# Row-max pass of an attention stage: next batches' work in half pieces, turns one batch further ahead, one score product issued twice

## What is computed

```python
def _attention(x, qkv_w, qkv_b, proj_w, proj_b):
    B, N, C = x.shape
    hd = C // HEADS                       # 12 heads of 16
    qkv = (x @ qkv_w + qkv_b).reshape(B, N, 3, HEADS, hd).transpose(2, 0, 3, 1, 4)
    q, k, v = (qkv[0], qkv[1], qkv[2])
    attn = jax.nn.softmax(jnp.einsum('bhnd,bhmd->bhnm', q, k) * hd ** (-0.5), axis=-1)
    o = jnp.einsum('bhnm,bhmd->bhnd', attn, v).transpose(0, 2, 1, 3).reshape(B, N, C)
    return o @ proj_w + proj_b
x = x + _attention(_layer_norm(x, ln1_g, ln1_b), qkv_w, qkv_b, proj_w, proj_b)
```

## Time and profile before

| | us |
|---|---|
| Median of 3 runs | 2577.85 (2576.46 to 2578.14) |
| Profiled execution, its own time | 2583.43 |
| Its span in the trace | 2581.4 |
| TensorE busy (matmuls) | 1948.3 (75%) |
| VectorE busy | 1506.0 (58%) |
| ScalarE busy | 1060.0 (41%) |
| Mean granted TensorE clock | 0.803 |

### The profile page before, as it was taken

The page is one execution under the profiler, slowest core; times in us unless marked ns, Lnnn a source line. Parts: engine busy times, 40 slices in busy tenths (PEclk is TensorE's granted clock), DMA queues, the critical chain, the costliest instruction groups (busy, mean ns, idle before and its releaser), DMA issues. The chain is left out here.

```text
span 2581.4 us, 31194 instructions
## 1 busy us (share of the span) xinstructions
PE 1948.3 (75%) x9560; PEld 1011.4 (39%) x9560; DVE 1506.0 (58%) x2508; ACT 1060.0 (41%) x1847; POOL 405.8 (16%) x592
## 2 busy tenths in 40 slices
PE   5687888868876351777568865788899994899994
PEld 4555645444334120000111123333123332788883
DVE  6376378843003665999757774788968886111113
ACT  2001122222111356999878863222167762222221
POOL 5000000000111000111100002522103335122221
PEclk9899989966886565555589986777589997899997
DMA  3011100051992003433000102977767742566664
GB/s 79 18 31 38 46 23 16 11 222 58 392 411 108 12 0 96 145 118 118 25 18 25 36 0 53 126 110 104 94 79 92 97 61 71 176 204 203 204 204 182
DMA packets 147741, 265.16 MB, mean 103 GB/s; under 512 B 28618, under 2 KB 115883, under 8 KB 142636
## 3 DMA queue, kind: packets, MB, share of 16 engines
q1 hardware_dynamic: 135996, 242.54, 36.3%
q0 software_dynamic: 10480, 18.04, 2.1%
q10 hardware_dynamic: 1152, 3.15, 0.3%
HBM read 221.85 MB, written 57.71 MB: 108 GB/s over the span
## 5 line engine op out<-in xcount | busy, mean ns | idle before, releaser
L1646 PE MATMUL ps<-arena 128*128 x384 | 195.8, 615 | 122.1 <-DMA arena<-arena 62.2
L1680 ACT ACTIVATE ps<-ps,arena 128x512 f32<-128x512 f32 x384 | 257.0, 1456 | 7.7 <-POOL arena L1666 7.7
L2091 DVE TENSOR_REDUCE arena<-ps 128x1024 f32 x192 | 227.7, 1222 | 50.4 <-PE ps L2241 44.4
L1656 DVE TENSOR_REDUCE arena<-ps 128x1024 f32 x192 | 234.7, 1226 | 38.1 <-PE ps L1646 22.1
L1680 ACT ACTIVATION_READ_ACCUMULATOR ps<-ps,arena 128x1 f32 x384 | 239.8, 1002 | 0.0
L2443 ACT ACTIVATE arena<-ps 128x1024 f32<-128x1024 f32 x192 | 185.2, 1022 | 95.7 <-PE ps L2325 94.6
L1830 ACT ACTIVATE arena<-ps 128x1024 f32<-128x1024 f32 x192 | 187.5, 1024 | 33.6 <-DVE arena L1852 29.4
L2773 DVE TENSOR_TENSOR arena<-ps,arena 128x384 f32<-128x384 f32 x39 | 21.8, 558 | 286.8 <-PE ps L2729 286.8
L2241 PE MATMUL ps<-arena 96*128 96x512 bf16 x384 | 159.6, 509 | 37.7 <-DVE arena L2091 25.6
L2753 ACT ACTIVATE arena<-ps,arena 128x256 f32<-128x256 f32 x234 | 89.7, 482 | 235.7 <-PE ps L2718 235.7
L528 PE MATMUL ps<-arena 96*128 96x456 f32 (+1 forms) x512 | 177.2, 500 | 9.6 <-DMA arena<-arena 6.1
(11 more groups left out here) (379 smaller groups left out, 3301.4 us busy)
## 6 DMA issues: line engine op xcount, KB each, us to landing
arena<-in_sm_w_dram SPq DMA_DIRECT2D x128, 576.0 KB
arena<-in_re_w_dram SPq DMA_DIRECT2D x39, 1252.0 KB, 5.9
arena<-ra_parts SPq DMA_DIRECT2D x192, 192.0 KB, 9.8
routed_in<-routed_in SPq DMA_DIRECT2D x8, 3332.0 KB, 14.3
ra_parts<-arena SPq DMA_DIRECT2D x48, 192.0 KB, 2.5
arena<-routed_in SPq DMA_DIRECT2D x39, 196.0 KB, 5.3
arena<-la_xt SPq DMA_DIRECT2D x16, 384.0 KB, 3.4
arena<-arena SPq DMA_DIRECT2D x64, 96.0 KB, 2.2
```

The source lines that it names most:

```text
L1646: ins = pe.matmul(ps[:, 2 * (n % 4) + t % 2, :], QM[j][:, h, t * P:(t + 1) * P], KI[:, b, h // HG, :], start=True, stop=True)
L1656: v.tensor_reduce(MXq[:, b, 2 * u:2 * u + 2, at_head(h)], ps[:, 2 * (n % 4):2 * (n % 4) + 2, :], AX.X, ALU.max).then_inc(s_lk, 1)
L1680: ins = act.activation(bank, bank, ACT.Exp, bias=nb[n % 4][:, t % 2:t % 2 + 1], scale=c_reg, accum_out=RS[:, b, t, at_head(h):at_head(h) + 1])
L2091: v.tensor_reduce(MX[:, bass.ds(b, 1), 2 * (n % 2):2 * (n % 2) + 2, n // 2].rearrange("p o t -> p (o t)"), ps[:, 2 * (n % 2):2 * (n % 2) + ...
```

## The change

Seven things are done in the row-max pass; what is computed stays the same.

1. `product` pieces are halved: each covers 256 of the 512 columns, so there are 16 of them. `turn` pieces are halved too (two transposes each).
2. The turns of a batch are made one batch earlier than the rest of its pieces: the pieces that run in batch b are the products and values of b + 2 and the turns of b + 3. The order is 16 half products, two values, four half turns, two values: 24 pieces, one for each unit, from unit 0.
3. The normalisation moves with them: `norm(b + 3)` in round b, with `norm(2)` ahead of the loop. `XT` has two buffers, so a second row is set to one.
4. ScalarE copies the turned rows of b + 1 behind the second part of b, ahead of the values copies of b (`turned`). Its loop is written out.
5. The banks 4 to 7 swap roles from batch to batch (`banks`).
6. In a unit, the first of the two score products is issued twice, into the same bank, but for the units 16, 17, 22 and 23, where the values pieces stand.
7. The first turns stand ahead of the pieces of batches 0 and 1.

```diff
--- before.py
+++ after.py
@@ -1967,7 +1967,7 @@
     Wp, bp = g2(P, [NG, D]), g2(P, [D])
     spare = g2(P, [1])
     mark = g2.at
-    XN, XT = g2(P, [T, D]), g2(DC + 1, [NC, S])
+    XN, XT = g2(P, [T, D]), [g2(DC + 1, [NC, S]) for _ in range(2)]
     QK = [g2(DC, [NC, S]) for _ in range(2)]
     PT = [[g2(DC, [NC, S], BF16) for _ in range(3)] for _ in range(2)]
     W, gb = g2(DC + 1, [NC, 3 * D]), g2(DC, [2, NC])
@@ -2017,7 +2017,8 @@
             l(v.reciprocal(ra, m.wk[2]))
             l(v.tensor_tensor(ra, ra, m.rstd, ALU.mult))
             v.wait_ge(s_w, 16 * (5 + HG))
-            v.memset(XT[DC:DC + 1, 0, :], 1.0)
+            for j in range(2):
+                v.memset(XT[j][DC:DC + 1, 0, :], 1.0)
 
         @block.scalar
         def _(act):
@@ -2036,6 +2037,7 @@
     ld = [sem(f"ra_stacks{j}_loaded") for j in range(2)]
     sl = [sem(f"ra_q_k_shift{j}_loaded") for j in range(2)]
     NLD = 2 * len(PAIRS)
+    banks = lambda b, k: 6 if (b + k) % 2 else 4
     NL2 = NLD + 3
     s_c, s_bt, s_bc = (sem(f"ra_shift_{n}") for n in ("parts", "turned", "copied"))
 
@@ -2094,10 +2096,11 @@
 
             norm(0)
             norm(1)
-            with v.Fori(0, B - 2) as b:
-                norm(b + 2)
+            norm(2)
+            with v.Fori(0, B - 3) as b:
+                norm(b + 3)
                 maxima(b, range(NU))
-            with v.Fori(B - 2, B) as b:
+            with v.Fori(B - 3, B) as b:
                 maxima(b, range(NU))
 
         @block.scalar
@@ -2106,12 +2109,16 @@
                 s.start(act)
             for k in range(2):
                 act.sem_inc(s_wr[k], 1)
-            with act.Fori(0, B) as b:
+
+            def turned(b):
                 xt.wait(act, b, 1)
                 for c in range(NC):
-                    ins = act.activation(XT[0:DC, c, :], ps[0:DC, 4 + c, :], ACT.Identity, bias=gb[:, 1, c:c + 1],
-                                         scale=gb[:, 0, c:c + 1])
+                    ins = act.activation(XT[b % 2][0:DC, c, :], ps[0:DC, banks(b, 0) + c, :], ACT.Identity,
+                                         bias=gb[:, 1, c:c + 1], scale=gb[:, 0, c:c + 1])
                 ins.then_inc(xc.sem, 1)
+
+            turned(0)
+            for b in range(B):
                 for k in range(2):
                     act.wait_ge(s_wr[k], 16 * 3 * b + 1)
                 for s in range(2 * NC):
@@ -2119,17 +2126,19 @@
                     if c == 0:
                         p2.wait(act, b, k - 1)
                     qp.wait(act, b, s + 1)
-                    bank = ps[0:DC, (6, 7, 4, 5)[s], :]
+                    bank = ps[0:DC, banks(b, k) + c, :]
                     act.activation(QK[k][:, c, :], bank, ACT.Copy)
                     act.activation(PT[k][0][:, c, :], bank, ACT.Copy).then_inc(qc.sem, 1)
                 for k in range(2):
                     rest.wait(act, b, k + 1)
                     act.activation(PT[k][1], QK[k], ACT.Copy).then_inc(p1.sem, 1)
+                if b + 1 < B:
+                    turned(b + 1)
                 qp.wait(act, b, 5)
-                Vb = V[:, bass.ds(b, 1), :].rearrange("p o (t h k d) -> p (o t) h k d", t=T, h=NH, k=2)
+                Vb = V[:, b, :].rearrange("p (t h k d) -> p t h k d", t=T, h=NH, k=2)
                 for u in range(2):
-                    ins = act.activation(Vb[:, 2 * u:2 * u + 2, :, 0, :],
-                                         ps[:, 6 + u, 0:2 * D].rearrange("p (t h d) -> p t h d", t=2, h=NH), ACT.Copy)
+                    ins = act.activation(Vb[:, 2 * u:2 * u + 2, :, 0, :], ps[:, banks(b, 0) + u, 0:2 * D].rearrange(
+                        "p (t h d) -> p t h d", t=2, h=NH), ACT.Copy)
                 ins.then_inc(vd.sem, 1)
             for u in range(AHEAD // 2):
                 act.wait_ge(s_bt, u + 1)
@@ -2202,23 +2211,26 @@
                 s.start(pe)
 
 
-            def turn(b, c):
-                if c == 0:
+            def turn(b, c, half):
+                if c == 0 and half == 0:
                     xn.wait(pe, b, 1)
                     qc.wait(pe, b, 0)
-                for t in range(T):
-                    ins = pe.transpose(ps[0:DC, 4 + c, t * P:(t + 1) * P], XN[:, t, c * DC:(c + 1) * DC], m.ident)
-                if c == NC - 1:
+                for t in (2 * half, 2 * half + 1):
+                    ins = pe.transpose(ps[0:DC, banks(b, 0) + c, t * P:(t + 1) * P], XN[:, t, c * DC:(c + 1) * DC],
+                                       m.ident)
+                if c == NC - 1 and half:
                     ins.then_inc(xt.sem, 1)
 
-            def product(b, s, c):
-                if s == 0 and c == 0:
-                    vd.wait(pe, b, 0)
-                    xc.wait(pe, b, 1)
-                rows = DC + 1 - c
-                ins = pe.matmul(ps[0:DC, (6, 7, 4, 5)[s], :], W[0:rows, c, s * DC:(s + 1) * DC], XT[0:rows, c, :],
-                                start=(c == 0), stop=(c == NC - 1))
-                if c == NC - 1:
+            def product(b, s, half, c):
+                if half == 0 and c == 0:
+                    if s == 0:
+                        xc.wait(pe, b, 1)
+                    elif s == NC:
+                        vd.wait(pe, b, 0)
+                rows, part = DC + 1 - c, slice(half * S // 2, (half + 1) * S // 2)
+                ins = pe.matmul(ps[0:DC, banks(b, s // NC) + s % NC, part], W[0:rows, c, s * DC:(s + 1) * DC],
+                                XT[b % 2][0:rows, c, part], start=(c == 0), stop=(c == NC - 1))
+                if half and c == NC - 1:
                     ins.then_inc(qp.sem, 1)
 
             def values(b, t):
@@ -2226,29 +2238,34 @@
                     qc.wait(pe, b, 2)
                 for c in range(NC):
                     rows = DC + 1 - c
-                    ins = pe.matmul(ps[:, 6 + t // 2, t % 2 * D:(t % 2 + 1) * D], XT[0:rows, c, t * P:(t + 1) * P],
-                                    W[0:rows, c, 2 * D:3 * D], start=(c == 0), stop=(c == NC - 1))
+                    ins = pe.matmul(ps[:, banks(b, 0) + t // 2, t % 2 * D:(t % 2 + 1) * D],
+                                    XT[b % 2][0:rows, c, t * P:(t + 1) * P], W[0:rows, c, 2 * D:3 * D],
+                                    start=(c == 0), stop=(c == NC - 1))
                 if t == T - 1:
                     ins.then_inc(qp.sem, 1)
 
-            pieces = [(turn, c) for c in range(NC)] + [(product, s, c) for s in range(2 * NC) for c in range(NC)] + \
-                [(values, t) for t in range(T)]
+            def pieces(b):
+                turns = [(turn, b + 1, c, half) for c in range(NC) for half in range(2)] if b + 1 < B else []
+                return [(product, b, s, half, c) for s in range(2 * NC) for half in range(2) for c in range(NC)] + \
+                    [(values, b, t) for t in range(2)] + turns + [(values, b, t) for t in range(2, T)]
 
             def scores(b, j, n):
                 h = n // 2
                 mx.wait(pe, b, n - 1)
-                for t in (2 * (n % 2), 2 * (n % 2) + 1):
+                first = 2 * (n % 2)
+                for t in (first, first + 1) if n in (16, 17, 22, 23) else (first, first, first + 1):
                     ins = pe.matmul(ps[:, t, :], ST_[j][0][0:KR, h, t * P:(t + 1) * P],
                                     ST_[j][1][0:KR, h, :], start=True, stop=True)
                 ins.then_inc(u1.sem, 1)
 
             def batch(b, ahead):
                 pe.wait_ge(ld[b % 2], 16 * NLD * (b // 2 + 1))
+                work = pieces(b + 2) if ahead else []
                 for n in range(NU):
                     scores(b, b % 2, n)
-                    if ahead and 0 < n <= len(pieces):
-                        piece, *which = pieces[n - 1]
-                        piece(b + 2, *which)
+                    if n < len(work):
+                        piece, *which = work[n]
+                        piece(*which)
                     at = (b - B + 2) * NU + n - 2
                     if 0 <= at < AHEAD * T // 2:
                         if at == 0:
@@ -2260,9 +2277,12 @@
                         if at % T == T - 1:
                             ins.then_inc(s_bt, 1)
 
+            for c in range(NC):
+                for half in range(2):
+                    turn(0, c, half)
             for b in range(2):
-                for piece, *which in pieces:
-                    piece(b, *which)
+                for piece, *which in pieces(b):
+                    piece(*which)
             for b in range(B):
                 batch(b, b + 2 < B)
 
```

## The result

The changed kernel takes 2567.02 us, median of nine runs (2562.74 to 2571.00), against 2578.14, also of nine, for the kernel before: a ratio of 0.9962 (95% interval 0.9951 to 0.9973), some 11 us less. It is faster by more than 0.2%, as forecast, but the gain is under a third of the 37 us expected, and 2567.02 lies outside the range of 2537 to 2556. The profiled execution took 2570.76 us (span 2568.7, mean granted clock 0.817), against 2583.43 (2581.4, 0.803).

What follows compares the result with a forecast made beforehand. The prediction took VectorE to become the bound after the change; its batch terms summed to 226.4 us against 263.4 for the pass, 37.0 us less, so 2577.85 - 37.0 gave 2541 us, range 2537 to 2556.

Steps and rivals of the forecast that it cites:

- its floor: Row-max pass: VectorE's row maximum needs 1.13 us a unit, 27.1 us a batch of 24 units.
- the margin of 0.05 us a unit: All units after the change: room under VectorE's 1.13 us; 0.1 us more per unit would cost 7 us over six batches.
- What was priced at nothing: Row-max pass: extra weight loads, DMA loads and stores, and ScalarE's copies were taken as covered, nothing charged.
- The normalisation, 1.15 us in batches 1 to 4: VectorE's four normalisation instructions, no longer hidden once VectorE is the bound, add 1.15 us to each of batches 1 to 4.
- (batch 0's is before the first score): Batch 0: its normalisation was placed ahead of the first score product, so nothing was charged for it.
- rival 3: Batches 1 to 4: normalisation meets POOL's late subtractions, 3.1 us four times, +12.5 us, 2553.5 us; chance 0.08.
- First batch's low clock, +2.5 us: Batch 0: scores start at clock 0.50, 1.0 us over the floor per unit for 2.5 units, +2.5 us.
- Does the clock hold?: Whole pass: three scores a unit, or two with a piece, were taken to keep TensorE's clock at 1.00.
- Rival 1: Batches 5 to 7: the clock falls and stays low, 1.445 us a unit, +8.5 or +13.5 us; chance 0.22.
- rival 4: Dense part of the batches: the clock stays down and the added columns make it slower, 2612 us; chance 0.03.
- the term of batches 6 and 7 in the sum: Batches 6 and 7: 27.1 and 28.4 us, all units under 1.13 us at 2.4 GHz.
- rival 2: Turn units of every batch: the clock falls there, 2.3 us five times, 12 us, 2553 us; chance 0.07.

Runs made afterwards that it cites:

- E2: Changed kernel with the first score product issued twice in every unit without a values piece, thin units included; ratio to the kernel before 0.9915.
- E1: Changed kernel with VectorE's normalisation moved from the head of the round to behind the twelfth row maximum; ratio to the kernel before 0.9930.
- E10: E5's kernel unchanged, profiled in another execution on the chip of E9; 2561.78 us.
- E11: E5's kernel unchanged, profiled in one more execution on the same chip as E10; 2581.13 us.
- after: The changed kernel itself, with all seven parts of the change and no further edit; 2567.02 us, ratio to the kernel before 0.9962.
- E3: Changed kernel with both E1's and E2's edits; ratio to the kernel before 0.9875.
- E7: Kernel before the change with only the second score issue added, in every unit without a piece; ratio to the kernel before 0.9918.
- E9: Changed kernel with E5's and E2's edits together; ratio to the kernel before 0.9869.
- E5: Changed kernel with POOL's three memsets moved earlier and VectorE's order kept; median 2550.69 us, ratio to the kernel before 0.9899.
- E4: Changed kernel without any second issue of a score product; ratio to the kernel before 0.9915.
- E6: Changed kernel with E1's normalisation and the second issue only in turn units and units without a piece; ratio to the kernel before 0.9893.

## Why the prediction was right or wrong

- **VectorE as the bound, its floor, the halves, the turns ahead: right.** Batches 1 to 4 were put at 28.3 us and take 28.3. A unit with a half product stays under the floor:

```profile
1663.57 0.82 PE L2257 MATMUL ps<-arena 96*128 96x512 bf16 x3
1664.23 0.59 PE L2231 MATMUL ps<-arena 96*96 96x256 f32 x2
1664.70 0.82 PE L2257 MATMUL ps<-arena 96*128 96x512 bf16 x3
```

  Three scores and a half product in 1.13 us, as priced (1.07 of work); the margin of 0.05 us a unit was enough, and weight loads cost nothing that shows.
- **What was priced at nothing: right.** In TensorE's groups within the pass the scores' idle time has 14.6 us for VectorE and 9.2 for a DMA, and the 9.2 are the single wait ahead of the first score; no product or turn waits:

```profile
L2257 PE MATMUL ps<-arena 96*128 96x512 bf16 x544 | 179.5, 448 | 27.6 <-DVE arena L2093 14.6 <-DMA arena<-ra_parts 9.2
L2231 PE MATMUL ps<-arena 97*96 97x256 f32 x192 | 59.1, 390 | 0.0
```

  So loads, stores and ScalarE's copies were covered.
- **The normalisation, 1.15 us in batches 1 to 4: right** (1.24 at 1660.01, batches of 28.3 against 27.2 without it, 27.23 for batches 5 to 7 in E2).
- **"(batch 0's is before the first score)": wrong, 8.9 us.** I placed the normalisation of batch 3 by its position in the program and did not follow what it waits for. It can begin only when the turns of batch 2 are done, beside POOL's chain of subtractions and memsets. The earlier trace rows had a neighbour at 4.39 us in just this place, and I used it as rival 3, in the wrong rounds (batches 1 to 4; ahead of the one at 1660.01 POOL was done at 1657.6) and with 3.1 us, the price beside subtractions of 2.1 us; beside memsets of 5.2 us each, every one of the four instructions can stand behind a whole one or more. The chance of 0.08 was for this mechanism elsewhere, so it does not count for it here. POOL's timeline around 1610 was the view that I didn't read.
- **First batch's low clock, +2.5 us: near.** Once its first maximum is done, batch 0 of E1 takes 30.1 us instead of the 28.4 of its others, which have a normalisation as well: 1.7 us. That 30.1 is so close to the 29.9 of the sum is in part luck: the sum had 0.8 us more for the clock and no normalisation there.
- **"Does the clock hold?": wrong, 16.4 us.** Rival 1 names the place (the thin units 22 and 23 at the end of batch 5) and has the right price for scores alone: 2.89 us for two units, measured 2.9. It came to 16.4 us and not 13.5 since a unit with two small transposes takes 1.72 us at 1.2 GHz, and I had 1.445 for all. The earlier trace rows had the price: eleven such units in 14.23 us are 1.29 each, and 0.43 for the second issue makes 1.72. The same row showed an engine that was busy without a gap at 0.50 and stayed there, so that the sentence under rival 4, by which every dense stretch in the rows brought the clock back, was not true of it. What failed is the term of batches 6 and 7 in the sum, 27.1 and 28.4 us at 2.4 GHz, where 36.8 and 35.1 were measured at 1.2 GHz, behind the two units at 1797.55 and 1798.68. I gave it 0.22 and the clock's holding 0.55. E10 and E11 show that the outcome of one execution was not to be had from the program alone; but all of after's nine runs have mean granted clocks of 0.814 to 0.821, where E2, E3, E7 and E9, in which the clock held, have 0.826 to 0.836, so the fall was its usual case. E5's four runs have 0.819 and 0.822 in the two longer ones and 0.826 and 0.831 in the two shorter. Only the profiled executions show the fall itself; that of the others is argued from these means.
- **Transposes at the end of a batch.** The turn units 18 to 21 of batches 1 to 4 kept the clock at 1.00 in after. The rule that spoke against them (the Trainium skill, TensorE: Matmul & The Clock Gate, Part 4: PE-mode transpose) did not decide here: rival 2 did not happen. In after each of these units has three score products beside its two transposes; E4 ran them with two, and there too the clock is 1.00 through all of them in batches 0 to 4. Its falls at 1663.1 and 1721.2 come behind product units, 1.8 and 1.3 us after TensorE's wait of 1.25 us for the normalisation:

```profile
1654.52 0.60 PE L2257 MATMUL ps<-arena 96*128 96x512 bf16 x2 [0.31 <-DVE arena L2093]
1654.96 0.38 PE L2219 MATMUL ps<-arena 128*96 128x128 f32 x2
...
1661.33 0.60 PE L2257 MATMUL ps<-arena 96*128 96x512 bf16 x2 [1.25 <-DVE arena L2093]
```

- **The chances and the range.** I treated the rivals as excluding each other. Rival 3's mechanism (8.9 us) and rival 1 (16.4) have nothing to do with each other and came together, 25 us (2541 + 8.9 + 16.4 = 2566.3, against 2567.02), and the range reached only to the worse of the single ones, 2556.
- **The second issue as part of the change.** I costed it at 2.4 GHz (nothing) and as rival 4 at 1.2 GHz in the dense part. That it makes the low state itself dearer, 0.43 us in 20 of 24 units, stood in rival 1's price; that a kernel without it would then be faster (E4) I did not draw from that.

**What stays open.** Why nearly all runs of after and E1 fall and about half of E5's do not, with the same instructions from batch 1 on. E5 differs in how long VectorE and TensorE wait at the beginning of the pass; no run here tells whether that matters or whether it is chance.

## What to carry to other kernels

When a change makes another engine the bound, go through every place where that engine has a small instruction that was hidden, the first round above all: what it waits for, and what its neighbour on the shared memory ports does in that moment. A filler that is to hold the clock has to cover the thinnest units, where no other work stands; here, where it left two of them in a row, the clock fell in nearly every execution of the changed kernel, as far as the mean clocks tell, and from then on the filler itself was part of what the stage had to pay for. Ask of rivals whether they can happen together, and let the range hold their sum.

## What the runs showed of the hardware that I had not expected

- A VectorE `tensor_scalar` of 128 x 192 stands behind whole POOL memsets: four instructions took 1.24 us with POOL idle, 5.3 to 5.6 beside subtractions, 11.00 beside subtractions and one memset of 5.2 us, and 20.84 beside subtractions and three such memsets. The row maxima hardly suffered: VectorE was busy 28.58 us in E1's batch 0 with 16.13 us of POOL beside it, and 28.30 in after's batch 1 with 9.73.
- With three score products every 1.13 us, 0.82 us of work and 0.31 idle each, the granted clock stayed 1.00 for the rest of the pass (E2, E7). Where it fell, units with two stood just ahead: those at 1797.55 and 1798.68 in after, and those around a wait of 1.25 us in E4 and E6. Such units are not always enough: in E5 and E10 the clock stayed through all of them.
- At 0.50 the engine can be busy nearly throughout and stay there: in after from 1800.35 to the end of the pass, with 16.46 of 17.00 us busy in its middle:

```profile
1814.00:1831.00 17.00, 16.46 (x44) 3.73 (x43) 13.22 (x11) 3.52 (x4) 0.00 (x0) 0.50 0.26 31
```

- The same kernel on the same chip took 2561.78 and 2581.13 us, and 16.8 of the 19.4 us between them lie in batches 5 to 7, around and behind the clock's fall. A single run of a kernel with such thin units says little.
